# The second normalisation of a two-layer kernel: statistics in halves, turns by tile, rotary products ahead of the last norm, tables loaded earlier

## The chip, the cores and the metric

The kernel runs on 1 core of one Trainium2 chip. The metric is the device time of one execution in microseconds (us), as the median of several runs. Engines: TensorE (PE, with its weight loads PEld), VectorE (DVE), ScalarE (ACT), GpSimd (POOL), and SyncE (SP), which only issues DMAs here. Each engine runs its own instructions in program order; semaphores order them between engines.

## The reference

Input x has 2048 tokens of 128 values. All is fp32.

```
xn = layernorm(x)
x  = x + token_memory(xn) + expert(xn)        # layer 0
xn = layernorm(x)                             # the second norm: this change
x  = x + attention(xn) + ffn(xn)              # layer 1
```

The attention of layer 1 has one head of 128 dimensions. q = xn Wq and k = xn Wk; of each, the first 64 dimensions are turned (rotary embedding) and the last 64 are skipped, that is, taken as they are:

```
even, odd = split(rot)                        # 32 + 32 of the 64 dimensions
rot' = [even*cos - odd*sin, even*sin + odd*cos]
q, k = [rot', skip] / sqrt(128)
p = softmax(q k^T, causal);  out = (p (xn Wv)) Wo
```

The ffn is tanh/silu-gated with two hidden layers of 512 and gelu.

## The kernel before, in words

Tokens stand in 16 tiles of 128, four tiles (512 tokens) make a chunk c = 0..3. Every engine has a hand-written list of steps; the order within an engine is the order in the code, and semaphores (`wait_ge`) are all that holds it against the others. Layer 0 ends at about 77 us with block b of the new x in PSUM bank b. What then happens, with the lines of the profile:

- ScalarE moves block b from PSUM to the tensor `x` (`first_block(b)`, L1247) in the order 1, 0, 2, 3. `x1_ready` counts them.
- VectorE takes the statistics of four tiles (`statistics`, L1905; for chunk 0 straight out of PSUM, L1898), aggregates them (`variances`, L1910); ScalarE takes the root (`deviations`, L1253); VectorE takes the reciprocal (L1916) and the shift -mean/deviation (`shifts`, L1917). Then the chunk is normalised into `xn`: tiles 0 and 1 by ScalarE (`normed`, L1260), tiles 2 and 3 by VectorE (L1922).
- TensorE transposes the four tiles (`normed`, L801), once all four are there, into PSUM; ScalarE copies the result to `xT` (`transposed`, L1264; `xt2_act` counts them).
- TensorE multiplies the chunk (`projected(c)`) with `wturn` (L810), `wswap` (L811: the same dimensions with the halves swapped) and `wskip` (L816). q and k stand side by side in the 128 columns of each.
- VectorE multiplies the first product by the cosine table (L1947) and the second by the sine table (L1949) into the buffer `TURN[c % 2]` (`rope_dve` counts), and adds the halves for q (L1951); GpSimd adds them for k (L1476). ScalarE copies the skipped dimensions (L1292, L1293). Behind it stand the masks in bf16 (L1299, L1300) and the fp16 high half of xT (L1268).
- From then on come the values (L826), and tile by tile the scores (L879), their maximum (L1981, VectorE), the exponential (L1354, ScalarE), the transposes (L892) and the weighted values (L902), with the ffn's gates (TensorE L852 and L853, tanh L1311, VectorE L1966, L1967 and, for most, the cast L1973, GpSimd's residue L1461 and L1462) laid between them by the lists `GATE_EARLY` and `GATE_LATE`. A gate u from 6 on waits for residue u-5 (`gate_low`, L1965). Then come the hidden layers (L929, L930).

Before the norm, SyncE has loaded the weights. It waits for `x1_ready` 2 and loads the tables `cosT` and `sinT`, 1 MB each, into a part of the arena that layer 0 has left by then; at `x1_ready` 4 it loads 1 MB of `h1_T`. GpSimd waits for `x1_ready` 4 too, and then makes fp16 casts of two weights (L1469, L1470) before its first k sum. VectorE computes some small products of scales (L1933 to L1937) between the last norm and the first rotary product.

In `projected(0)` the transposes of chunk 1 stand between the swapped and the skipped product; those of chunks 2 and 3 come after the skipped products of chunks 0 and 1:

```python
            normed(0)
            keep_warm(4, 7)
            for c in range(4):
                ...
                projected(c)
                for n in ((2,), (3,), (), ())[c]:
                    normed(n)
            values(0)
```

Of the kernel before, what the change touches and what calls it, by code (L numbers as in the profile page):

```python
# [6 lines left out]
ALU = mybir.AluOpType  # L7
ACT = mybir.ActivationFunctionType
AX = mybir.AxisListType
# [4 lines left out]
P = 128  # L14
# [72 lines left out]
def program(nc, a, out):  # L87
    with ExitStack() as ctx:
# [42 lines left out]
        s1, s2, sh1, sh2, s1h, s12 = (take(HT4) for _ in range(6))  # L131
        a_tab = at[0]
        HT = take(2 * T).rearrange("p (h t) -> p h t", h=2)
        cosT, sinT = arena[:, a_tab:a_tab + T], arena[:, a_tab + T:a_tab + 2 * T]
        a_blocks = at[0]
# [16 lines left out]
        Gf = take((HALF + 1) * S)  # L152
        G = Gf.rearrange("p (j s) -> p j s", j=HALF + 1)
        CC = take(3 * (L + 1) * L).rearrange("p (q j t) -> p q j t", q=3, j=L + 1)

# [6 lines left out]
        STf = take(SCAN * RW)  # L162
        VC = take(HALF * L).rearrange("p (j t) -> p j t", j=HALF)
        O1, O2, O3, O4, TA, TB, TC = (take(HALF * L).rearrange("p (j t) -> p j t", j=HALF) for _ in range(7))
        Yf = take(L * L)
# [73 lines left out]

        TURN = [hBf[:, T * c:T * c + 2 * BANK].rearrange("p (k t) -> p k t", k=2) for c in range(2)]  # L240
        xd = hBf[:, T + 2 * BANK:T + 3 * BANK]
# [184 lines left out]
        def _(sp):  # L426
# [16 lines left out]

            sp.wait_ge(x1_ready, 2)
            for i, n in enumerate(("cos", "sin")):
                sp.dma_start((cosT, sinT)[i], a[n]).then_inc(tab_in, 16)

# [52 lines left out]
        def _(pe):  # L500
# [293 lines left out]
            def normed(c):  # L794
                b = 4 * ((c + 1) % 2)
                pe.wait_ge(xn2_act, 2 * c + 2)
                pe.wait_ge(xn2_dve, 2 * c + 2)
                if c >= 2:
                    pe.wait_ge(xt2_act, c - 1)
                for n in range(4 * c, 4 * c + 4):  # L800
                    i = tr(PS[:, b, (n % 4) * P:(n % 4 + 1) * P], xn[:, n, :], ident)  # L801
                i.then_inc(xrt_done, 1)

            def projected(c):
                b = 4 * ((c + 1) % 2)
                xc = xT[:, c * BANK:(c + 1) * BANK]
                pe.wait_ge(xt2_act, c + 1)
                if c >= 2:
                    pe.wait_ge(rope_dve, 2 * c - 2)
                mm(bank(b + 2), wturn, xc, start=True, stop=True).then_inc(turn_done, 1)  # L810
                mm(bank(b + 3), wswap, xc, start=True, stop=True).then_inc(turn_done, 1)  # L811
                if c == 0:
                    normed(1)
                if c >= 2:
                    pe.wait_ge(skip_act, 2 * c - 2)
                mm(bank(b + 1), wskip, xc, start=True, stop=True).then_inc(skip_done, 1)  # L816
# [14 lines left out]
            for c in range(4):  # L831
                if c == 1:

                    pe.wait_ge(x1_ready, 4)
                projected(c)
                for n in ((2,), (3,), (), ())[c]:
                    normed(n)
            values(0)
# [174 lines left out]
        def _(act):  # L1013
# [241 lines left out]
            def normed(c):  # L1255

                act.wait_ge(x1_ready, max(c + 1, 2))
                act.wait_ge(shift_ready, c + 1)
                for n in range(4 * c, 4 * c + 2):
                    f(xn[:, n, :], x[:, n, :], ACT.Identity, scale=lnt[:, 1, n:n + 1], bias=lnt[:, 6, n:n + 1]).then_inc(xn2_act, 1)  # L1260
# [8 lines left out]

            first_block(1)  # L1270
            deviations(0)
            first_block(0)
            normed(0)
            first_block(2)
            deviations(1)
            transposed(0)
            first_block(3)
            normed(1)
            deviations(2)
            normed(2)  # L1280
            transposed(1)
            deviations(3)
            normed(3)
            transposed(2)

            f(small[:, 38:39], lnt[:, 0, 12:13], ACT.Tanh)
            for c in range(4):

                b = 4 * ((c + 1) % 2)
                cols = slice(c * BANK, (c + 1) * BANK)  # L1290
                act.wait_ge(skip_done, c + 1)
                f(qT1[0:ROT, cols], PS[0:ROT, b + 1, :], ACT.Copy).then_inc(skip_act, 1)  # L1292
                f(kT1[0:ROT, cols], PS[ROT:P, b + 1, :], ACT.Copy).then_inc(skip_act, 1)  # L1293
                if c == 0:
                    transposed(3)
                if c == 2:
                    act.wait_ge(xt2_act, 1)
                    high(0)
                    f(ident_b, ident, ACT.Copy).then_inc(mask_act, 1)  # L1299
                    f(causal_b, con[:, C_CAUSAL:C_CAUSAL + P], ACT.Copy).then_inc(mask_act, 1)  # L1300
            act.wait_ge(xt2_act, 4)
# [217 lines left out]
        def _(dve):  # L1519
# [380 lines left out]

            def statistics(b):

                dve.wait_ge(x1_ready, b if b == 1 else b + 1)
                for n in range(4 * b, 4 * b + 4):
                    did(v.bn_stats(st[:, n, :], x[:, n, :]))  # L1905
# [13 lines left out]
            def normed(c):  # L1919
                dve.wait_ge(x1_ready, max(c + 1, 2))  # L1920
                for n in range(4 * c + 2, 4 * c + 4):
                    v.tensor_scalar(xn[:, n, :], x[:, n, :], mv[:, n, 0:1], lnt[:, 1, n:n + 1], ALU.subtract, ALU.mult).then_inc(xn2_dve, 1)  # L1922

            first_variances()
            for c in range(4):
                shifts(c)
                normed(c)
                if c < 3:
                    statistics(c + 1)
                    variances(c + 1)  # L1930

            dve.wait_ge(small_in, 16 * 13)
            v.tensor_scalar(s1h, s1, 0.5, None, ALU.mult).then_inc(scales_ready, 1)  # L1933
            v.scalar_tensor_tensor(out=s12, in0=s1, scalar=0.5, in1=s2, op0=ALU.mult, op1=ALU.mult).then_inc(scales_ready, 1)
            need(did(v.tensor_tensor(s12a, s1, s2, ALU.mult)))
            v.tensor_reduce(sums[:, 0:1], s12a, AX.X, ALU.add, apply_absolute_value=True).then_inc(sums_ready, 1)
            v.tensor_reduce(sums[:, 1:2], sh1, AX.X, ALU.add, apply_absolute_value=True).then_inc(sums_ready, 1)  # L1937

            dve.wait_ge(tab_in, 32)
            for c in range(4):  # L1940
                b = 4 * ((c + 1) % 2)
# [6 lines left out]
                dve.wait_ge(turn_done, 2 * c + 2)  # L1948
                v.tensor_tensor(TURN[c % 2][:, 1, :], bank(b + 3), sinT[:, cols], ALU.mult).then_inc(rope_dve, 1)  # L1949
                dve.wait_ge(rope_dve, 2 * c + 2)  # L1950
                v.tensor_tensor(qT1[ROT:P, cols], TURN[c % 2][0:ROT, 0, :], TURN[c % 2][0:ROT, 1, :], ALU.add).then_inc(turned_dve, 1)  # L1951

            def values(c):
# [156 lines left out]
```

## Time and profile before

| what | value |
|---|---|
| runs | 259.75, 259.87, 261.55 us, median 259.87 |
| profiled execution: span from its first to its last instruction | 258.2 us |
| profiled execution: its own time | not listed apart from the span |
| TensorE busy | 245.4 us (95%) |
| VectorE busy | 206.3 us (80%) |
| ScalarE busy | 186.8 us (72%) |
| GpSimd busy | 112.7 us (44%) |
| mean granted TensorE clock | 0.992 of full |
| DMA | 8.50 MB in the whole kernel |

Busy time is the time in which an engine executes; register, semaphore and DMA-issuing instructions don't count. Idle time of an engine costs something only where another one waits for it. Durations overlap where instructions are pipelined: a row with "x2" gives the time from the start of the first to the end of the second. The end of a TensorE instruction is modelled; its starts are recorded.

### The profile page before, as it was taken

How to read it: one execution, taken by the hardware profiler on the slowest of the kernel's cores; microseconds unless marked ns; L12 is line 12 of the kernel's file. 1: busy time of each engine (PE TensorE's matmuls, PEld its weight loads, DVE VectorE, ACT ScalarE, POOL GpSimd, SP SyncE). 2: the span in 40 equal slices, each digit the busy share in tenths (PEclk: the TensorE clock that was granted, in tenths of full speed). 3: DMA queues.
4: the chain of work that ended last, by engine and by line, in shares of the span. 5: the costliest groups of instructions: out<-in, count | busy, mean ns of one | idle time of the engine just before them, and what ended most of it. 6: DMA issues, size and time to landing. Idle time of an engine off the chain costs nothing.

```text
span 258.2 us, 5143 instructions
## 1 busy us (share of the span) xinstructions
PE 245.4 (95%) x1665; PEld 160.8 (62%) x1665; DVE 206.3 (80%) x694; ACT 186.8 (72%) x459; POOL 112.7 (44%) x148
## 2 busy tenths in 40 slices
PE   7798799999999999999999999999999999999993
PEld 2257554567674458688777767976975444444482
DVE  5998789999968898998899896897623897666684
ACT  1588499986637797887757899989923997777730
POOL 9698300000001689988655795987880000000000
PEclk9999799999999999999999999999999999999999
DMA  7720000000004704000000000000000000000004
GB/s 198 198 57 3 0 1 3 1 0 3 1 1 175 316 3 164 3 0 1 4 0 3 0 0 0 5 0 3 0 0 3 0 0 0 3 3 0 0 30 139
DMA packets 8303, 8.50 MB, mean 33 GB/s; under 512 B 1745, under 2 KB 7378, under 8 KB 7762
## 3 DMA queue, kind: packets, MB, share of 16 engines
q1 hardware_dynamic: 7442, 7.65, 9.1%
q10 hardware_dynamic: 832, 0.49, 0.7%
q8 instruction: 15, 0.25, 0.4%
q14 instruction: 14, 0.11, 0.2%
HBM read 7.09 MB, written 1.05 MB: 32 GB/s over the span
## 4 chain that ended last, share of the span: by engine, by line
PE 66%; DVE 16%; POOL 8%; ACT 4%; issue 3%; DMA 2%; DVEq 0%; SPq 0%; POOLq 0%; ACTq 0%
PE PS L930 11%; PE PS L929 11%; PE PS L902 8%; PE PS L879 7%; PE PS L892 4%; POOL arena L1461 4%; POOL arena L1462 3%; PE PS L693 3%; PE PS L646 3%; PE PS L701 2%; DMA x<-L_attn_x 2%; DVE mxb L1981 2%; DVE arena L1967 2%; PE PS L530 2%; PE PS L685 1%
## 5 line engine op out<-in xcount | busy, mean ns | idle before, releaser
L929 PE MATMUL PS<-arena 128*128 128x512 f16 x128 | 48.5, 379 | 0.0
L930 PE MATMUL PS<-arena 128*128 128x512 f16 x128 | 48.5, 379 | 0.0
L2039 DVE TENSOR_TENSOR arena<-arena 128x512 f32<-128x512 f32 x32 | 22.2, 693 | 13.0 <-ACT arena L1385 13.0
L879 PE MATMUL PS<-arena 128*128 128x512 f32 (+3 forms) x80 | 31.9, 530 | 0.3 <-ACT arena L1354 0.3
L1384 ACT ACTIVATE arena<-PS,arena 128x512 f32<-128x512 f32 x32 | 22.9, 716 | 9.1 <-PE PS L930 9.1
L1461 POOL TENSOR_TENSOR arena<-arena 128x256 f32<-128x256 f32 x32 | 21.6, 674 | 15.4 <-DVE arena L1973 12.9
L1354 ACT ACTIVATE arena<-PS,lnt 128x512 f32<-128x512 f32 (+3 forms) x40 | 24.8, 628 | 2.9 <-DVE lnt L1988 2.8
L1462 POOL TENSOR_TENSOR arena<-arena,small 128x256 f16<-128x256 f32 (+1 forms) x36 | 23.8, 662 | 2.8
L1469 POOL CAST arena<-arena 128x512 f16<-128x512 f32 x2 | 1.3, 636 | 54.3 <-ACT x L1247 54.3
L1385 ACT ACTIVATE arena<-PS,arena 128x512 f16<-128x512 f32 x32 | 22.8, 713 | 0.0
L1981 DVE TENSOR_REDUCE mxb<-PS 128x1 f32<-128x512 f32 (+3 forms) x40 | 22.1, 601 | 0.0
L930 PEld LDWEIGHTS PS<-arena 128*128 128x128 f16 x128 | 12.5, 98 | 14.7
L929 PEld LDWEIGHTS PS<-arena 128*128 128x128 f16 x128 | 12.5, 98 | 14.6
L879 PEld LDWEIGHTS PS<-arena 128*128 128x128 f32 x80 | 14.0, 191 | 12.0 <-issue 9.8
L892 PE MATMUL PS<-con,arena 128*128 128x128 f32 x136 | 19.5, 273 | 0.0
L902 PE MATMUL PS<-arena,xn 128*128 128x128 f32 x144 | 19.3, 278 | 0.0
L902 PEld LDWEIGHTS PS<-arena,xn 128*128 128x128 f32 x144 | 17.7, 191 | 1.1 <-ACT xn L1338 0.2
L902 PE MATMUL PS<-arena 128*128 128x128 f32 x128 | 17.3, 278 | 0.6 <-ACT arena L1338 0.6
L2010 DVE SCALAR_TENSOR_TENSOR x<-PS,lnt,x 128x128 f32<-128x128 f32 x16 | 5.6, 351 | 14.2 <-PE PS L902 13.6
L892 PEld LDWEIGHTS PS<-con,arena 128*128 128x128 f32 x136 | 15.1, 141 | 2.7 <-issue 1.9
L902 PEld LDWEIGHTS PS<-arena 128*128 128x128 f32 x128 | 15.6, 191 | 1.3 <-ACT arena L1338 1.0
L1967 DVE SCALAR_TENSOR_TENSOR arena<-PS,arena 128x256 f32<-128x256 f32 x32 | 15.5, 484 | 1.1
(291 smaller groups left out, 615.5 us busy)
## 6 DMA issues: line engine op xcount, KB each, us to landing
arena<-h_T SPq DMA_DIRECT2D x2, 1024.0 KB, 6.3
x<-L_attn_x SPq DMA_DIRECT2D x4, 256.0 KB, 4.7
arena<-cos SPq DMA_DIRECT2D x1, 1024.0 KB, 4.8
arena<-sin SPq DMA_DIRECT2D x1, 1024.0 KB, 7.8
arena<-w_T SPq DMA_DIRECT2D x3, 256.0 KB, 3.3
out<-arena SPq DMA_DIRECT2D x2, 256.0 KB, 2.2
con<-shape_constants ACTq DMA_DIRECT2D x1, 192.5 KB, 3.5
out<-arena SPq DMA_DIRECT2D x1, 192.0 KB, 2.0
```

Of the source, the lines that this page charges most:

```text
L879: i = mm(PS[:, k, 0:cnt * P], qT1[:, t * P:(t + 1) * P], kT1[:, c * P:(c + cnt) * P], start=True, stop=not last)
L892: i = tr(PS[:, 4 + gi % 2, (b - c) * P:(b - c + 1) * P], Pr[t % 2][:, b * P:(b + 1) * P], ident)
L902: i = mm(PS[:, 7, (t % 4) * D:(t % 4 + 1) * D], PT[t % 2][:, b * P:(b + 1) * P], V1[:, b, :], start=(b == 0), stop=(b == t))
L929: mm(bank(b), wH[:, k, m * P:(m + 1) * P], sH[:, k, cols], start=(k == 0), stop=False)
L930: i = mm(bank(b), wL[:, k, m * P:(m + 1) * P], sL[:, k, cols], start=False, stop=(k == HT4 - 1))
L1354: f(Pr[t % 2][:, c * P:(c + cnt) * P], PS[:, SCORE_BANK[gi], 0:cnt * P], ACT.Exp, scale=1.0 / D, bias=nbs[:, t:t + 1], accum_out=rsums[:, ...
L1384: f(FP[u % 4], bank(u % 8), ACT.Gelu, scale=s_[:, u % HT4:u % HT4 + 1])
L1385: f(high, bank(u % 8), ACT.Gelu, scale=s_[:, u % HT4:u % HT4 + 1]).then_inc(read, 1)
L1461: o.need(o.did(tt(rest, value, high, ALU.subtract)))
L1462: return tt(low, rest, low_scale.broadcast_to([P, cols]), ALU.mult)
L1981: i = did(v.tensor_reduce(mxb[:, gi:gi + 1], PS[:, SCORE_BANK[gi], 0:cnt * P], AX.X, ALU.max))
L2039: v.tensor_tensor(RP[m], FP[m], high, ALU.subtract).then_inc(rest_ready, 1)
```

## The change

Seven edits, all around the second norm:

1. `cosT` and `sinT` move to places in the arena that layer 0 leaves earlier; SyncE loads the cosines once `lanes_act` is 8 and the sines once `tables_ready` is 1 and `terms_act` is 2 (in the trace of before, about 34 to 40 us). VectorE waits for both tables before the norm's loop. The buffers `TURN` move to another place.
2. VectorE: two of the next chunk's four statistics stand between the aggregation of a chunk and its reciprocal, where it waits for ScalarE's root; the other two after the chunk's norm. For the last chunk the two rotary products of chunk 0 stand there.
3. VectorE: the rotary sum is a step of its own; the small products of scales come after rotary chunk 1.
4. ScalarE: blocks move in the order 1, 2, 0, 3, and the steps in a new order: each turned block is copied earlier, the skipped copies of chunk 0 come before the last norm.
5. TensorE transposes tile by tile, in the order 2, 0, 3, 1, each with a wait of its own.
6. TensorE: the transposes of chunk c+1 stand between the swapped and the skipped product of chunk c, for c = 0, 1, 2.
7. Waits on `x1_ready` follow the new order of the blocks.

```diff
+        cosT = Gf[:, S:S + T]
...
+        sinT = arena[:, at[0]:at[0] + T]
...
-        TURN = [hBf[:, T * c:T * c + 2 * BANK].rearrange("p (k t) -> p k t", k=2) for c in range(2)]
+        TURN = [hAf[:, 2 * T + 2 * BANK * c:2 * T + 2 * BANK * (c + 1)].rearrange("p (k t) -> p k t", k=2) for c in range(2)]
...
-            sp.wait_ge(x1_ready, 2)
-            for i, n in enumerate(("cos", "sin")):
-                sp.dma_start((cosT, sinT)[i], a[n]).then_inc(tab_in, 16)
+            sp.wait_ge(lanes_act, 8)
+            sp.dma_start(cosT, a["cos"]).then_inc(tab_in, 16)
+            sp.wait_ge(tables_ready, 1)
+            sp.wait_ge(terms_act, 2)
+            sp.dma_start(sinT, a["sin"]).then_inc(tab_in, 16)
...
             def normed(c):
                 b = 4 * ((c + 1) % 2)
-                pe.wait_ge(xn2_act, 2 * c + 2)
-                pe.wait_ge(xn2_dve, 2 * c + 2)
                 if c >= 2:
                     pe.wait_ge(xt2_act, c - 1)
-                for n in range(4 * c, 4 * c + 4):
+                for k in range(4):
+                    n = 4 * c + (2, 0, 3, 1)[k]
+                    pe.wait_ge(xn2_act if k % 2 else xn2_dve, 2 * c + k // 2 + 1)
                     i = tr(PS[:, b, (n % 4) * P:(n % 4 + 1) * P], xn[:, n, :], ident)
...
-                if c == 0:
-                    normed(1)
+                if c < 3:
+                    normed(c + 1)
...
-                for n in ((2,), (3,), (), ())[c]:
-                    normed(n)
```

ScalarE's steps before and after (`skipped(c)` is the pair of copies L1292, L1293; it was a loop over c before):

```
before: block 1, root 0, block 0, norm 0, block 2, root 1, turned 0, block 3,
        norm 1, root 2, norm 2, turned 1, root 3, norm 3, turned 2, tanh (table load),
        skipped 0, turned 3, skipped 1, skipped 2, high 0, masks, skipped 3, high 1
after:  block 1, block 2, root 0, block 0, norm 0, turned 0, root 1, norm 1,
        block 3, root 2, turned 1, norm 2, root 3, skipped 0, turned 2, norm 3,
        tanh (table load), skipped 1, turned 3, skipped 2, high 0, masks, skipped 3, high 1
```

VectorE's after:

```diff
+            first_variances()
+            dve.wait_ge(tab_in, 32)
+            for c in range(4):
+                if c < 3:
+                    statistics(c + 1, 0)
+                else:
+                    rotated(0)
+                shifts(c)
+                normed(c)
+                if c < 3:
+                    statistics(c + 1, 1)
+                    variances(c + 1)
+
+            rotary_sum(0)
+            rotated(1)
+            rotary_sum(1)
+            dve.wait_ge(small_in, 16 * 13)
...
+            for c in range(2, 4):
+                rotated(c)
+                rotary_sum(c)
```

`statistics(b, half)` waits for `x1_ready` 1, 2 or 4 (b = 1, 2, 3) and takes two tiles.

## Rows read from the trace of the kernel before

**Rows 1.** Windows: us, busy by engine (instructions), PEclk, DMA share, GB/s.

```profile
82.30:88.00 5.70, 5.64 (x19) 2.72 (x20) 4.80 (x32) 3.99 (x11) 4.17 (x4) 1.00 1.01 425
96.00:103.00 7.00, 7.00 (x55) 5.83 (x55) 6.03 (x18) 5.23 (x15) 6.41 (x6) 1.00 0.46 151
```

**Rows 2.** The chain that ended last: start, us, engine, tile, line.

```profile
116.66 0.62 POOL arena L1462
...
117.33 0.43 DVE arena L1966
```

**Rows 3.** VectorE (DVE) timeline: start, us, line, operation [idle before <-releaser].

```profile
80.13 0.86 DVE L1905 BATCH_NORM_STATS2 st<-x 128x6 f32<-128x128 f32 x4
81.03 0.38 DVE L1910 BATCH_NORM_AGGREGATE mv<-st 128x2 f32<-128x6 f32 x4
81.78 0.18 DVE L1916 RECIPROCAL lnt<-lnt 128x4 f32<-128x4 f32 x1 [0.36 <-ACT lnt L1253]
...
82.58 0.87 DVE L1905 BATCH_NORM_STATS2 st<-x 128x6 f32<-128x128 f32 x4
...
87.55 0.15 DVE L1934 SCALAR_TENSOR_TENSOR arena<-arena 128x4 f32<-128x4 f32 x1
...
87.94 0.68 DVE L1947 TENSOR_TENSOR arena<-PS,arena 128x512 f32<-128x512 f32 x1
...
89.26 0.68 DVE L1951 TENSOR_TENSOR arena<-arena 64x512 f32<-64x512 f32 x1
...
96.09 0.29 DVE L1981 TENSOR_REDUCE mxb<-PS 128x1 f32<-128x128 f32 x1
...
101.73 0.42 DVE L1966 SCALAR_TENSOR_TENSOR arena<-arena,PS 128x256 f32<-128x256 f32 x1 [0.42 <-ACT arena L1311]
```

**Rows 4.** Timeline of TensorE (PE), the same columns.

```profile
80.55 0.66 PE L801 MATMUL PS<-con,xn 128*128 128x128 f32 x4 [0.42 <-ACT xn L1260]
...
82.28 1.13 PE L810 MATMUL PS<-xT,arena 128*128 128x512 f32 x2 [0.21 <-ACT xT L1264]
...
84.10 0.60 PE L801 MATMUL PS<-con,xn 128*128 128x128 f32 x4
84.54 1.02 PE L816 MATMUL PS<-xT,arena 128*128 128x512 f32 x2
...
92.13 1.02 PE L810 MATMUL PS<-xT,arena 128*128 128x512 f32 x2
...
95.59 0.39 PE L879 MATMUL PS<-arena 128*128 128x128 f32 x2
```

**Rows 5.** Timeline of ScalarE (ACT), the same columns.

```profile
82.13 0.59 ACT L1247 ACTIVATE x<-PS 128x512 f32<-128x512 f32 x1
...
87.14 0.88 ACT L1260 ACTIVATE xn<-x,lnt 128x128 f32<-128x128 f32 x2 [0.50 <-DVE lnt L1917]
...
88.52 1.28 ACT L1286 ACT_TABLE_LOAD   x1
...
89.92 0.58 ACT L1292 ACTIVATE arena<-PS 64x512 f32<-64x512 f32 x1
...
91.14 0.60 ACT L1264 ACTIVATE xT<-PS 128x512 f32<-128x512 f32 x1
```

**Rows 6.** Timeline of GpSimd (POOL), the same columns.

```profile
85.56 1.48 POOL L1470 TENSOR_SCALAR arena<-arena 128x512 f16<-128x512 f32 x1
89.37 1.70 POOL L1476 TENSOR_TENSOR arena<-arena 64x512 f32<-64x512 f32 x1 [2.33 <-DVE arena L1949]
...
97.34 1.17 POOL L1461 TENSOR_TENSOR arena<-xT,arena 128x512 f32<-128x512 f32 x1
```

**Rows 7.** Timeline of VectorE in the attention.

```profile
165.09 1.18 DVE L1973 CAST arena<-arena 128x256 f16<-128x256 f32 x1
```

**Rows 8.** Timeline of GpSimd in the attention.

```profile
164.85 1.28 POOL L1496 TENSOR_TENSOR arena<-arena 128x512 f32<-128x512 f32 x1
```

**Rows 9.** DMA issues: KB each, median us from issue to landing.

```profile
arena<-sin SPq DMA_DIRECT2D x1, 1024.0 KB, 7.8
```

More of the change, by code:

```diff
@@ L131, in program @@
         s1, s2, sh1, sh2, s1h, s12 = (take(HT4) for _ in range(6))
-        a_tab = at[0]
         HT = take(2 * T).rearrange("p (h t) -> p h t", h=2)
-        cosT, sinT = arena[:, a_tab:a_tab + T], arena[:, a_tab + T:a_tab + 2 * T]
         a_blocks = at[0]
@@ L1255, in normed @@
             def normed(c):
-                act.wait_ge(x1_ready, max(c + 1, 2))
+                act.wait_ge(x1_ready, max(c + 1, 3))
                 act.wait_ge(shift_ready, c + 1)
@@ L1268, in high, with skipped @@
                 f(xH[:, c * BANK:(c + 1) * BANK], xT[:, c * BANK:(c + 1) * BANK], ACT.Copy).then_inc(xh_act, 1)
[L1270 to L1287, printed above, removed]
+            def skipped(c):
                 b = 4 * ((c + 1) % 2)
@@ L1293, in _ @@
                 f(kT1[0:ROT, cols], PS[ROT:P, b + 1, :], ACT.Copy).then_inc(skip_act, 1)
[L1294 to L1300, printed above, removed]
+            first_block(1)
+            first_block(2)
+            deviations(0)
+            first_block(0)
+            normed(0)
+            transposed(0)
+            deviations(1)
+            normed(1)
+            first_block(3)
+            deviations(2)
+            transposed(1)
+            normed(2)
+            deviations(3)
+            skipped(0)
+            transposed(2)
+            normed(3)
+            f(small[:, 38:39], lnt[:, 0, 12:13], ACT.Tanh)
+            skipped(1)
+            transposed(3)
+            skipped(2)
+            act.wait_ge(xt2_act, 1)
+            high(0)
+            f(ident_b, ident, ACT.Copy).then_inc(mask_act, 1)
+            f(causal_b, con[:, C_CAUSAL:C_CAUSAL + P], ACT.Copy).then_inc(mask_act, 1)
+            skipped(3)
             act.wait_ge(xt2_act, 4)
@@ L1899, in first_variances, with statistics @@
                 variances(0)
-            def statistics(b):
-                dve.wait_ge(x1_ready, b if b == 1 else b + 1)
-                for n in range(4 * b, 4 * b + 4):
+            def statistics(b, half):
+                dve.wait_ge(x1_ready, (1, 2, 4)[b - 1])
+                for n in range(4 * b + 2 * half, 4 * b + 2 * half + 2):
                     did(v.bn_stats(st[:, n, :], x[:, n, :]))
@@ L1919, in normed, with rotated @@
             def normed(c):
-                dve.wait_ge(x1_ready, max(c + 1, 2))
+                dve.wait_ge(x1_ready, max(c + 1, 3))
                 for n in range(4 * c + 2, 4 * c + 4):
                     v.tensor_scalar(xn[:, n, :], x[:, n, :], mv[:, n, 0:1], lnt[:, 1, n:n + 1], ALU.subtract, ALU.mult).then_inc(xn2_dve, 1)
[L1924 to L1940, printed above, removed]
+            def rotated(c):
                 b = 4 * ((c + 1) % 2)
@@ L1949, in _, with rotary_sum @@
                 v.tensor_tensor(TURN[c % 2][:, 1, :], bank(b + 3), sinT[:, cols], ALU.mult).then_inc(rope_dve, 1)
+            def rotary_sum(c):
+                cols = slice(c * BANK, (c + 1) * BANK)
                 dve.wait_ge(rope_dve, 2 * c + 2)
                 v.tensor_tensor(qT1[ROT:P, cols], TURN[c % 2][0:ROT, 0, :], TURN[c % 2][0:ROT, 1, :], ALU.add).then_inc(turned_dve, 1)
+            first_variances()
[14 more added lines that the diff above has]
+            dve.wait_ge(small_in, 16 * 13)
+            v.tensor_scalar(s1h, s1, 0.5, None, ALU.mult).then_inc(scales_ready, 1)
+            v.scalar_tensor_tensor(out=s12, in0=s1, scalar=0.5, in1=s2, op0=ALU.mult, op1=ALU.mult).then_inc(scales_ready, 1)
+            need(did(v.tensor_tensor(s12a, s1, s2, ALU.mult)))
+            v.tensor_reduce(sums[:, 0:1], s12a, AX.X, ALU.add, apply_absolute_value=True).then_inc(sums_ready, 1)
+            v.tensor_reduce(sums[:, 1:2], sh1, AX.X, ALU.add, apply_absolute_value=True).then_inc(sums_ready, 1)
+            for c in range(2, 4):
+                rotated(c)
+                rotary_sum(c)
             def values(c):
```

## The prediction

> **What bounds the kernel now.** I read the windows of busy time first. From 96 to 103 us TensorE is busy 7.00 of 7.00 us at granted clock 1.00, while VectorE has 6.03 [rows 1]. So what follows the change is TensorE's, with some waits on VectorE, and the changed stretch (77 to 96 us) is worth what it brings forward TensorE's first scores. The chain of waits says otherwise: from 97 to 117 us it runs through GpSimd's residues and then into the gate of line 1966 [rows 2]. I take these links for coincidence. By the code gate u waits for residue u-5. The gate at 117.33 is u = 9 (two gates a tile from tile 2 on), so it wants four residues, and the one that ends at 117.28 is the seventh.
>
> Then the three engines' timelines of the norm. VectorE repeats a pattern every 2.45 us (80.13 to 82.58): four statistics 0.90, four aggregations 0.39, an idle 0.36 while ScalarE takes the root, then reciprocal, shift and two norms 0.80. It goes into the rotary products at 87.94 and takes the first maximum at 96.09 [rows 3]. TensorE's turns and projections start at 82.28 and stand almost back to back until the first scores at 95.59 [rows 4]. Both are thus tight at 96: scores end about 0.45 after their start, just when VectorE has finished.
>
> **VectorE, part by part.** Removed: the idle 0.36 behind each root. Two statistics cost 0.45 and fill it, three times; the first pair of rotary products, 2 x 0.60 by the distance of 87.94 to the next but one at 89.26, fills the fourth. That is 4 x 0.36 = 1.44 at most. Given back: (a) ScalarE now copies chunk 0's turned block before root 1. The turn can end about 80.85 (its last tile is ScalarE's second norm, ready 80.5 [rows 4]), so the 0.60 copy ends 81.45 and the root runs 81.4 to 81.7; VectorE, at 81.4, idles 0.2 to 0.3. (b) Block 3's move out of PSUM now stands behind norm 1 (about 82.9 to 83.5 instead of 82.13 to 82.73 [rows 5]), and VectorE at 83.3 wants it for the first half of chunk 3: 0.15. Together 0.4 to 0.5. So the reciprocal of chunk 3 falls at 86.7 although 1.2 us of rotary work has been done before it (86.67 in the pattern of before), and all VectorE work to the last rotary sum would end at 96.09 - 0.95 = 95.1.
>
> **TensorE.** Before, the four transposes start at 80.55, when ScalarE's last norm is there. Turning by tile leaves one of the four behind it; the four warming matmuls follow at once and chunk 0's projection starts about 81.5 instead of 82.28, with the copy of 80.85 to 81.45 just in time. A chunk then costs 1.82 (82.28 to 84.10, turned and swapped projection) + 0.44 (transposes) + 0.92 (the skipped projection, half of 1.82 and a little) = 3.2 us [rows 4]. Three chunks bring TensorE to 91.1, where it wants the turned block of chunk 3. That block comes from ScalarE.
>
> **ScalarE.** Here I see the end of the gain. Before, the order is norm 3, copy 2, table load at 88.52 (1.28), the two skipped copies of chunk 0 from 89.92, copy 3 at 91.14 [rows 5]. After, it is root 3, skipped copies 0 (85.7 to 87.0), copy 2 (about 87.15), norm 3 (87.65, two of 0.88 together), table load, skipped copies of chunk 1, copy 3. Skipped copies 0 take the place in which ScalarE idled before; norm 3 is 0.5 later than at 87.14, but copy 2 now stands ahead of it and not behind. The table load thus comes at 88.5 as before, and copy 3 at 89.9 + 1.22 = 91.12, as before, ending 91.7. What was late before was TensorE (92.13); now it waits and starts chunk 3 at 91.75. The gain there is 0.38 us of the 0.76 that TensorE had at chunk 0. From there to the scores the work is unchanged (92.13 to 95.59 is 3.46): 95.21. The masks and the high half, behind skipped copies 2, are ready near 94.2, in time.
>
> **GpSimd, and a shared resource.** Line 1476 adds 64 partitions in 1.70 us where line 1461 adds 128 in 1.17; it starts 0.1 after VectorE's own sum of line 1951 (0.68), which has two inputs in SBUF [rows 3, 6]. The difference, 0.53, is about what is left of VectorE's sum. The opposite order shows too: the cast of line 1973 at 165.09 takes 1.18, where line 1966 handles the same 128x256 shape in 0.42 [rows 3], and ends 0.14 after the GpSimd instruction that was running since 164.85 [rows 7, 8]. So whichever comes second waits. Bounds for what the change meets of it: nothing, and one GpSimd addition of 1.17 us for each time that VectorE comes second. It can come second twice. Sum 0 is due at 87.55, while GpSimd's weight casts, 0.7 later than before with block 3, run to 87.75: 0.2. The scale products of lines 1934 and 1935 (two SBUF inputs) stood at 87.5, with GpSimd idle [rows 3]; now they come at 90.5, just when sum 1 lets GpSimd's second addition go: up to 1.15. I take 0.2 and, for the second, most of 1.15; VectorE's 0.95 is then spent, and it reaches the first maximum at about 96.05.
>
> The Trainium skill says this as a rule ("SBUF — State Buffer", Who interferes with whom): a VectorE instruction with two SBUF inputs and a GpSimd instruction that reads SBUF exclude each other, and the first to issue decides. The two rows agree with it; that tiny instructions pay a whole GpSimd instruction is what it adds, and no row of before has it. Without the rule VectorE would be free at 95.1 and wait for the scores.
>
> **The sum.** With no collision all engines pass 96 us 0.38 us earlier, TensorE setting it: VectorE's 0.95 is cut to TensorE's 0.38. With the collisions the first maximum gains only 0.04; but VectorE had a wait of 0.42 at 101.73 on a tanh that itself follows TensorE [rows 3], so it catches up most of TensorE's lead. I take 0.3 us. Behind 102 us everything moves by this, and nothing there changes except the chance phase of VectorE and GpSimd (a cast that waits 0.9 us or not [rows 7]), worth some 0.2 either way by my estimate. The loads are worth nothing: the sine table lands 7.8 us after its issue at 79.6 [rows 9], so at 87.4, covered by the norm (no idle at 87.94), and it is now loaded 40 us earlier. The span was 258.2 us; the runs' median, 259.87, lies 1.67 above it, which I keep (the profiled execution's own time is not listed). 258.2 - 0.3 + 1.67 = 259.57.
>
> **Rivals.**
> 1. ScalarE's order doesn't bind and the stretch gains what VectorE gains: 0.95 to 1.2 us, 258.8. For it: VectorE is the visible chain of this stretch. Against: two engines were tight at 96 us, and copy 3 keeps its place.
> 2. GpSimd takes the port first at sum 0 too. VectorE's sum is ready at 87.55 and GpSimd's next addition may start from 87.85; if VectorE comes more than 0.3 us later than I reckon, sum 0 waits 1.17 more. VectorE then ends at 97.2, 1.1 later than before, of which some 0.4 is caught up at 101.73: 0.5 to 0.9 slower, 260.5. Up to that 0.3 us the change is a gain, from it on a loss. For it: rotary products ahead of norm 3 leave no slack; against: only the phase decides.
> 3. The tables' loads, 2 MB inside the token chain (35 to 45 us), delay its short instructions or their fetching. Two of the three 1 MB loads fill the share of 1.01 that 82.3 to 88 us shows [rows 1], so one takes about 2.8 us, and a fetch behind one could wait as long: 262.6. Against: under that full DMA the copy of line 1247 took 0.59 [rows 5] and VectorE kept its 2.45 us.
> 4. The change doesn't do what it says: the roots are held by ScalarE's copies so that the idle only moves. Then chunk 3 is 0.5 late and copy 3 with it: 260.0.
>
> **How the numbers follow.** Forecast as above 0.55 (its own range 259.2 to 259.8); rival 1 0.17; rival 2 0.13; rival 3 0.05; rival 4 0.10. The 8-in-10 range reaches from near rival 1 to near rival 2: 258.7 to 260.4. One per cent, 2.6 us, is what a measurement of this kernel can tell from no change; only rival 3 reaches it, and no sum of gains does. So faster 0.02, same 0.93, slower 0.05.
>
> **What would show it.** Right: statistics in pairs with no idle of 0.36 behind the aggregations; chunk 0's projection near 81.5; TensorE idle 0.5 to 0.7 before chunk 3's projection, released by ScalarE's line of the turned copy; scores near 95.2; a scale product of over 1 us near 90.5. Wrong: no such idle in TensorE (rival 1), the first rotary sum over 1.5 us long and the first maximum near 97 (rival 2), long instructions or idle at 35 to 45 us (rival 3), recurring idle behind the roots (rival 4).

## The result, and the profile after

| kernel | median of the runs | range | runs |
|---|---|---|---|
| before | 260.06 us | 258.92 to 261.62 | 17 |
| changed | 261.39 us | 261.01 to 262.80 | 17 |

The ratio is 1.0051, with a 95% interval of 1.0031 to 1.0071: the change costs 0.5%, some 1.3 us. The forecast was 259.57 with a range of 258.7 to 260.4: a small gain was expected, and a loss beyond the range came.

The executions of every kernel here fall into groups 1.0 to 1.7 us apart by TensorE's granted clock, which differs ahead of the norm (in the profiles here, 0.91 to 1.00 from 30 to 58 us), so medians are given as well for the "clock group", the runs with a mean clock of 0.9875 to 0.9935. In that group the changed kernel has 261.12 us (9 runs) and the kernel before 259.88 to 260.06 (10 to 22 runs in each set of experiments): 1.1 to 1.2 us. Inside the profiles I count from the norm's first statistics, which leaves out what differs ahead of it.

The tables' loads cost little if anything. They are now issued at 30.77 and 37.82 us and take 4.7 us each, inside the token chain, and the norm starts at 77.43 against 77.46 us before. The granted clock moves that start too, so a fairer pair is the kernel before with late scale products (below), which loads the tables at the old place: its norm starts at 77.25 with a clock of 0.94 from 30 to 58 us, as the changed kernel has it. So up to some 0.2 us can't be ruled out.

The page of the changed kernel, its head and its busy times:

```profile
span 259.3 us, 5142 instructions
...
PE 245.9 (95%) x1665; PEld 160.0 (62%) x1665; DVE 208.5 (80%) x694; ACT 186.8 (72%) x459; POOL 112.0 (43%) x148
```

VectorE is busy 2.2 us longer than before with the same 694 instructions. So some instructions took longer, and the timeline of VectorE shows where (start, us, line, operation, shapes; the lines to compare are [rows 3]):

```profile
78.65 0.45 DVE L1909 BATCH_NORM_STATS2 st<-x 128x6 f32<-128x128 f32 x2
...
84.24 0.98 DVE L1926 TENSOR_SCALAR xn<-x,mv,lnt 128x128 f32<-128x128 f32 x2
...
85.94 0.66 DVE L1936 TENSOR_TENSOR arena<-PS,arena 128x512 f32<-128x512 f32 x1
86.52 0.68 DVE L1938 TENSOR_TENSOR arena<-PS,arena 128x512 f32<-128x512 f32 x1
87.11 0.17 DVE L1920 RECIPROCAL lnt<-lnt 128x4 f32<-128x4 f32 x1
...
88.02 1.66 DVE L1944 TENSOR_TENSOR arena<-arena 64x512 f32<-64x512 f32 x1
89.72 0.69 DVE L1936 TENSOR_TENSOR arena<-PS,arena 128x512 f32<-128x512 f32 x1
...
91.04 0.68 DVE L1944 TENSOR_TENSOR arena<-arena 64x512 f32<-64x512 f32 x1
91.76 1.12 DVE L1963 TENSOR_SCALAR arena<-arena 128x4 f32<-128x4 f32 x1
...
97.25 0.29 DVE L2001 TENSOR_REDUCE mxb<-PS 128x1 f32<-128x128 f32 x1
...
102.76 0.42 DVE L1986 SCALAR_TENSOR_TENSOR arena<-arena,PS 128x256 f32<-128x256 f32 x1 [0.42 <-ACT arena L1315]
```

The idle of 0.36 us behind the aggregations is filled, as it was meant to be (78.65 stands in it; only ahead of chunk 1's reciprocal 0.33 is left), and the reciprocal of chunk 3 comes at 87.11. But three rows are too long. The first rotary sum takes 1.66 us; the same instruction at 91.04 takes 0.68. The first scale product, 128x4 elements, takes 1.12 where it took 0.16 before. The pair of norms at 84.24 takes 0.98 where it takes 0.60 elsewhere, and the next instruction starts 0.90 behind it instead of 0.51. These are 0.98, 0.96 and 0.38 us more, together 2.3 for the 2.2 of the page. Beside them stands the timeline of GpSimd of the same kernel:

```profile
84.27 1.50 POOL L1474 TENSOR_SCALAR arena<-arena 128x512 f16<-128x512 f32 x1
...
86.31 1.48 POOL L1474 TENSOR_SCALAR arena<-arena 128x512 f16<-128x512 f32 x1
87.88 1.26 POOL L1480 TENSOR_TENSOR arena<-arena 64x512 f32<-64x512 f32 x1
91.08 1.76 POOL L1480 TENSOR_TENSOR arena<-arena 64x512 f32<-64x512 f32 x1 [1.95 <-DVE arena L1938]
```

The k sum of 87.88 started 0.14 us before VectorE's q sum of 88.02 and ran to 89.14; that of 91.08 started just behind VectorE's sum of 91.04, took half a microsecond longer than the first and ran to 92.84, and the scale product issued at 91.76 ended at 92.88. VectorE ends its rotary work at 97.22 instead of 96.07 and takes the first maximum at 97.25 instead of 96.09.

The timelines of TensorE and ScalarE in the changed kernel:

```profile
81.54 1.11 PE L813 MATMUL PS<-xT,arena 128*128 128x512 f32 x2
...
92.13 1.13 PE L813 MATMUL PS<-xT,arena 128*128 128x512 f32 x2 [0.72 <-ACT xT L1265]
...
95.70 0.39 PE L880 MATMUL PS<-arena 128*128 128x128 f32 x2
...
98.48 0.30 PE L893 MATMUL PS<-con,arena 128*128 128x128 f32 x1 [0.67 <-DVE arena L1975]
```

```profile
86.06 0.30 ACT L1254 ACTIVATE lnt<-mv,small 128x4 f32<-128x4 f32 x1 [0.71 <-DVE mv L1914]
...
88.86 1.28 ACT L1296 ACT_TABLE_LOAD   x1
...
91.48 0.60 ACT L1265 ACTIVATE xT<-PS 128x512 f32<-128x512 f32 x1
```

TensorE starts chunk 0's projection 0.74 earlier than before [rows 4] and has lost all of it at chunk 3, for whose turned block from ScalarE it waits 0.72. The scores come at 95.70, 0.1 later than before. Then it waits 0.67 more at 98.48, for VectorE's copy of the values. The gate at 102.76 is 1.03 later than in [rows 3], counted from the norm 1.06, and it stays so: the last of this line's 32 instructions starts at 187.43, 1.08 after the 186.35 of the kernel before.

### The profile page after: what moved, and what is told of

It is laid out like the page before. It is cut to its first block, busy times and chain, and to the rows that moved or that the text cites. A ratio compares the mean times of both kernels' runs of the same rounds, so it can differ in the third digit from the quotient of the medians.

```text
span 259.3 us, 5142 instructions
## 1 busy us (share of the span) xinstructions
PE 245.9 (95%) x1665; PEld 160.0 (62%) x1665; DVE 208.5 (80%) x694; ACT 186.8 (72%) x459; POOL 112.0 (43%) x148
## 4 chain that ended last, share of the span: by engine, by line
PE 71%; DVE 17%; ACT 6%; issue 2%; DMA 2%; SPq 0%; DVEq 0%; ACTq 0%
PE PS L930 11%; PE PS L931 11%; PE PS L903 9%; PE PS L880 9%; PE PS L893 5%; PE PS L695 3%; PE PS L648 3%; DVE arena L1987 2%; PE PS L703 2%; DVE arena L1986 2%; DMA x<-L_attn_x 2%; DVE mxb L2001 2%; PE PS L854 2%; PE PS L853 2%; PE PS L532 2%
```

## The experiments

Two theories stood against each other. PORT: VectorE and GpSimd hold each other up for whole instructions, and the new order has put three of VectorE's instructions second. (The name is a label: the traces show the waits, not a port.) ORDER: the new order on ScalarE and TensorE makes the last turned block late, and VectorE's delay only follows. In the tables "max" is the first maximum of the scores, "gate" the first gate product, both in us from the norm's first statistics in the one profiled execution, "end" the end of the span counted so; "median" is that of the runs in the clock group named above. Every ratio is against the kernel before, run in the same set.

| kernel | scores | max | gate | end | median (runs) |
|---|---|---|---|---|---|
| before | 18.13 | 18.63 | 24.27 | 180.74 | 259.9 to 260.06 |
| changed | 18.27 | 19.82 | 25.33 | 181.87 | 261.12 (9) |
| changed, scale products early | 18.26 | 18.75 | 24.40 | 181.31 | 260.74 (6) |
| changed, k sum second | 18.26 | 18.98 | 24.56 | 181.21 | 260.53 (6) |
| changed, products behind the norm | 18.27 | 19.51 | 25.02 | 181.63 | 260.87 (9) |
| before, scale products late | 18.13 | 19.71 | 25.22 | 181.85 | 261.09 (6) |
| both repairs | 18.26 | 18.74 | 24.40 | 181.28 | 260.48 (7) |
| both, new ScalarE order | 17.37 | 17.85 | 23.54 | 179.84 | 259.00 (7) |
| ... and early weight casts | 17.07 | 17.55 | 23.23 | 180.04 | 259.31 (6) |
| ... and GpSimd 0.3 us later | 17.07 | 17.55 | 23.23 | 179.66 | 258.93 (7) |
| both, new order, products behind | 18.00 | 18.48 | 24.17 | 180.54 | 259.75 (6) |

The experiments are of three sets on three chips, and in each the kernel before has a median of its own: 260.06 for the four kernels under "changed", 259.90 for the next three, 259.88 for the last two. Distances between sets are best read from these.

**The kernel before, with one edit.** The five scale products move from ahead of rotary chunk 0 to behind rotary chunk 1. Nothing else of the change is in it.

```diff
-            dve.wait_ge(small_in, 16 * 13)
-            v.tensor_scalar(s1h, s1, 0.5, None, ALU.mult).then_inc(scales_ready, 1)
...
                 v.tensor_tensor(qT1[ROT:P, cols], TURN[c % 2][0:ROT, 0, :], TURN[c % 2][0:ROT, 1, :], ALU.add).then_inc(turned_dve, 1)
+                if c == 1:
+                    dve.wait_ge(small_in, 16 * 13)
+                    v.tensor_scalar(s1h, s1, 0.5, None, ALU.mult).then_inc(scales_ready, 1)
...
```

> The kernel before with one edit: the scale products stand behind the sum of rotary chunk 1 instead of ahead of chunk 0. The work is the same. PORT: the first of them waits for GpSimd's second k sum, 1.0 to 1.1 us, first maximum at 97.1, total 0.8 to 1.1 over the kernel before. ORDER: within 0.2 of the kernel before.

Measured: 261.12 us, ratio 1.0036 (1.0009 to 1.0063); in the clock group 1.03 over the kernel before. First the row of the kernel before, then VectorE and GpSimd of this one:

```profile
87.48 0.16 DVE L1933 TENSOR_SCALAR arena<-arena 128x4 f32<-128x4 f32 x1
```

```profile
90.74 0.69 DVE L1944 TENSOR_TENSOR arena<-arena 64x512 f32<-64x512 f32 x1
91.46 1.12 DVE L1947 TENSOR_SCALAR arena<-arena 128x4 f32<-128x4 f32 x1
92.50 0.15 DVE L1948 SCALAR_TENSOR_TENSOR arena<-arena 128x4 f32<-128x4 f32 x1
...
96.96 0.29 DVE L1981 TENSOR_REDUCE mxb<-PS 128x1 f32<-128x128 f32 x1
```

```profile
90.79 1.77 POOL L1476 TENSOR_TENSOR arena<-arena 64x512 f32<-64x512 f32 x1 [0.27 <-DVE arena L1942]
```

The same scale product of 0.16 us takes 1.12 as soon as it stands behind a q sum, with nothing else changed. Its end and GpSimd's (90.79 + 1.77 = 92.56) tell the mechanism: it ends 0.02 after GpSimd. This single move costs the kernel before nearly as much as the whole change does. The wait on GpSimd is thus shown, and shown to be enough for such a loss; ORDER had expected at most 0.2.

**The changed kernel, scale products early.** They move into VectorE's wait for `count_done`, ahead of the norm, where GpSimd is idle.

```diff
+            dve.wait_ge(small_in, 16 * 13)
+            v.tensor_scalar(s1h, s1, 0.5, None, ALU.mult).then_inc(scales_ready, 1)
...
             dve.wait_ge(count_done, 1)
```

> The changed kernel, its five small scale products moved ahead of the norm, into VectorE's wait for the last count of layer 0. Theory PORT (whichever of VectorE and GpSimd comes second waits for the other's whole instruction): the scale product of 1.12 us and the 0.4 us behind it leave the stretch, VectorE is free 1.5 us earlier, so at 95.7, and the first maximum falls to the scores' end, about 96.2 instead of 97.25; total 0.9 to 1.1 us under the changed kernel, so 0.2 to 0.4 over the kernel before. Theory ORDER (the new order on ScalarE and TensorE makes the last turned block late, and VectorE's delay is only a follower): scores stay at 95.7, and the gain is at most the 0.46 us of moved work.

Measured: 260.77 us, ratio 1.0027 (1.0001 to 1.0053). VectorE in this kernel, whose norm starts at 76.39:

```profile
86.97 1.67 DVE L1951 TENSOR_TENSOR arena<-arena 64x512 f32<-64x512 f32 x1
...
95.14 0.29 DVE L2001 TENSOR_REDUCE mxb<-PS 128x1 f32<-128x128 f32 x1 [0.37 <-PE PS L882]
...
100.79 0.42 DVE L1986 SCALAR_TENSOR_TENSOR arena<-arena,PS 128x256 f32<-128x256 f32 x1 [0.42 <-ACT arena L1315]
```

The maximum is at the scores' end, 18.75 from the norm, and the gate is 0.93 earlier than in the changed kernel, as PORT had it, although the q sum still takes 1.67. But the total is only 0.4 to 0.6 better, not the 0.9 to 1.1 expected: against the kernel before, the maximum of tile 6 is 0.13 late and that of tile 7 is 0.57. The cause is taken up below.

**The changed kernel, k sum second.**

```diff
                 pool.wait_ge(rope_dve, 2 * c + 2)
+                pool.wait_ge(turned_dve, c + 1)
                 tt(kT1[ROT:P, cols], TURN[c % 2][ROT:P, 0, :], TURN[c % 2][ROT:P, 1, :], ALU.add).then_inc(turned_pool, 1)
```

> The changed kernel, GpSimd's k sum of a chunk held until VectorE's q sum of that chunk is done. PORT: the first q sum takes 0.68 instead of 1.66 us; GpSimd's sums take about 1.2 instead of 1.8 us, so GpSimd loses nothing. The scale products then stand at 90.7, with GpSimd's second sum just let go: still one wait of about 1 us there. First maximum about 96.3, total 0.7 to 1.0 under the changed kernel. ORDER: no gain, as GpSimd only starts later.

Measured: 260.66 us, ratio 1.0024 (0.9993 to 1.0055), 0.59 under the changed kernel in the clock group, where 0.7 to 1.0 was expected. VectorE and GpSimd:

```profile
87.98 0.69 DVE L1945 TENSOR_TENSOR arena<-arena 64x512 f32<-64x512 f32 x1
...
90.74 0.17 DVE L1964 TENSOR_SCALAR arena<-arena 128x4 f32<-128x4 f32 x1
90.82 0.15 DVE L1965 SCALAR_TENSOR_TENSOR arena<-arena 128x4 f32<-128x4 f32 x1
90.89 1.24 DVE L1966 TENSOR_TENSOR small<-arena 128x4 f32<-128x4 f32 x1
...
96.37 0.29 DVE L2002 TENSOR_REDUCE mxb<-PS 128x1 f32<-128x128 f32 x1
```

```profile
88.84 1.27 POOL L1481 TENSOR_TENSOR arena<-arena 64x512 f32<-64x512 f32 x1 [1.10 <-DVE arena L1945]
90.85 1.26 POOL L1481 TENSOR_TENSOR arena<-arena 64x512 f32<-64x512 f32 x1 [0.74 <-DVE arena L1945]
```

GpSimd's sum takes 1.27 instead of 1.77 us when it doesn't overlap VectorE's. The explicit wait isn't free for GpSimd, though: its sum ends 1.41 to 1.44 us behind VectorE's, against 1.13 in the kernel before. The q sum is back at 0.69. Of the scale products the first two slip through before GpSimd starts at 90.85; the third (`s1 * s2`, two inputs in SBUF), issued 0.04 after it, takes 1.24. That the same scale product right behind a q sum takes 0.17 here also rules out that it waits for the q sum itself. The wait was expected; that it falls on whichever instruction comes after GpSimd's start, on one with two SBUF inputs here and on one with a single input in the other runs, is what these two runs show together.

**The changed kernel, rotary products of chunk 0 behind the last norm.**

```diff
-                else:
-                    rotated(0)
...
+            rotated(0)
             rotary_sum(0)
```

> The changed kernel, the rotary products of chunk 0 back behind the last norm. PORT: the q sum comes right behind its products, before GpSimd, and takes 0.68 us; VectorE loses the filled root wait of 0.4 but gains 1.0: first maximum 96.6 or better, total 0.4 to 0.8 under the changed kernel. ORDER: total unchanged or 0.4 over the changed kernel.

Measured: 260.87 us, ratio 1.0011 (0.9987 to 1.0036); in the clock group 0.25 under the changed kernel, less than the 0.4 to 0.8 expected. VectorE:

```profile
86.44 0.33 DVE L1921 SCALAR_TENSOR_TENSOR lnt<-mv,lnt 128x4 f32<-128x4 f32 x1
86.70 1.02 DVE L1926 TENSOR_SCALAR xn<-x,mv,lnt 128x128 f32<-128x128 f32 x2
...
88.52 0.68 DVE L1944 TENSOR_TENSOR arena<-arena 64x512 f32<-64x512 f32 x1
...
91.28 1.13 DVE L1962 TENSOR_SCALAR arena<-arena 128x4 f32<-128x4 f32 x1
```

The q sum is at 0.68 and the scale product still waits (1.13), both as expected. The last norm's pair now takes 1.02 beside GpSimd's weight work of 86.15. That row looks worse than it is, for the next instruction starts 0.51 behind it, as behind any pair. Most of what eats the gain of 0.98 is that VectorE sits idle 0.37 for the last root again, and that the shift ahead of the norm takes 0.33 instead of 0.16 beside GpSimd, which delays the norm by 0.18.

**Both repairs.** Scale products early and k sum second together.

> The changed kernel with both repairs: scale products ahead of the norm and GpSimd's k sum behind VectorE's q sum. PORT: VectorE is free near 94.7 instead of 97.22 and waits for the scores, which stay at 95.7 because TensorE waits for the last turned block; first maximum about 96.2, at most 0.1 from the run with the scale products moved alone. So the 1.0 us of the q sum is worth nothing once TensorE is the last. Behind it a difference of up to 0.5 from the phase of GpSimd. ORDER: the same. This run tells what bounds the stretch once the collisions are gone.

Measured: 260.56 us, ratio 1.0028 (1.0000 to 1.0056); one of its twelve executions took 362.86 us at a mean granted clock of 0.654, why is not known, and of the numbers here it is only in the 260.56. Maximum and gate are those of the run with the scale products alone, to 0.01. VectorE is free at 95.55 (its last rotary sum starts at 94.86 and takes 0.69; 94.7 was expected) and the scores are what it waits for. So the second microsecond was hidden behind TensorE: the two waits of 1.0 us on VectorE did not add, and each repair alone recovers 0.77 and 0.93 of the 1.06 at the gate. What is left is 0.13 at the gate, which is TensorE's late scores (0.13, too), and 0.4 more at tile 6. So even without these two waits the changed kernel is no faster than the kernel before: the 0.38 us that TensorE was to gain isn't there either.

**Both repairs and a new order on ScalarE.**

```diff
-            skipped(1)
             transposed(3)
+            skipped(1)
```

> Both repairs, and on ScalarE the copy of the last turned block ahead of the skipped copies of chunk 1. If TensorE's wait of 0.72 before chunk 3 is the bound that is left, the scores come 0.6 to 0.8 earlier than in the run with both repairs, at about 95.0, the maximum at about 95.5, and the total falls 0.4 to 0.8 under the kernel before, less what the phase of GpSimd takes. If something else bounds (the skipped copies, the masks), nothing moves.

Measured: 259.25 us, ratio 0.9985 (0.9955 to 1.0015). This interval shows no difference; in the clock group it is 259.00 us (7 runs, 258.87 to 259.28) against 259.90 (13 runs, 259.70 to 260.07), without overlap. TensorE and ScalarE (this profile's norm starts at 78.86):

```profile
92.67 1.11 PE L813 MATMUL PS<-xT,arena 128*128 128x512 f32 x2
...
96.23 0.39 PE L880 MATMUL PS<-arena 128*128 128x128 f32 x2
```

```profile
90.28 1.28 ACT L1296 ACT_TABLE_LOAD   x1
...
92.01 0.60 ACT L1265 ACTIVATE xT<-PS 128x512 f32<-128x512 f32 x1 [0.23 <-PE PS L804]
```

TensorE's wait before chunk 3 is gone, and scores come 0.89 earlier than with both repairs, somewhat more than the 0.6 to 0.8 expected; the cast at tile 6, taken up below, gives back another 0.44. ORDER, dead as a cause of the loss, is thus the cause of the missing gain: two copies of 0.6 us stood between the table load and the block for which TensorE waited.

**Early weight casts.** On top of that:

```diff
-            pool.wait_ge(x1_ready, 4)
+            pool.wait_ge(x1_ready, 1)
             for wH, wL, w in ((w1H, w1L, w1T), (w2H, w2L, w2T)):
```

> As the run before it, and GpSimd's weight casts released by the first moved block instead of the fourth, so at 77.9 instead of 83.7. PORT: VectorE's first norm of chunk 2 loses its wait (0.98 for the pair instead of 0.60), root 3 and all behind it come 0.4 earlier, unless the casts now hit the norm of chunk 0 or 1 instead. Expect 0.1 to 0.4 us under the run before it; if the casts only move the collision, no difference.

Measured: 259.93 us, ratio 0.9987 (0.9957 to 1.0017). The gate is 0.31 earlier and the pair of norms is back at 0.60, as expected; yet the total is 0.2 (by the end in the profile) to 0.3 us (by the clock group) worse than in the run before. Outside the clock group the medians of the two kernels are equal (260.65 and 260.64), so the traces carry the argument here and not the medians. The norms of chunks 0 and 1, which now stand beside the casts, take 0.63 and 0.60, so the collision was not moved to them. The loss is again at tile 6, where VectorE casts for the first time. VectorE, and GpSimd at that moment:

```profile
85.47 0.60 DVE L1934 TENSOR_SCALAR xn<-x,mv,lnt 128x128 f32<-128x128 f32 x2
...
120.31 0.80 DVE L1994 CAST arena<-arena 128x256 f16<-128x256 f32 x1
```

```profile
120.28 0.67 POOL L1465 TENSOR_TENSOR arena<-arena 128x256 f32<-128x256 f32 x1
```

The cast, issued 0.03 us after GpSimd had started, takes 0.80. In the kernel before, the same cast took its least:

```profile
120.16 0.29 DVE L1973 CAST arena<-arena 128x256 f16<-128x256 f32 x1
```

```profile
119.67 0.61 POOL L1462 TENSOR_TENSOR arena<-arena,small 128x256 f16<-128x256 f32 x1
120.43 0.67 POOL L1461 TENSOR_TENSOR arena<-arena 128x256 f32<-128x256 f32 x1
```

It was issued when GpSimd's instruction had 0.12 us left. Over the nine kernels seen so far, the first cast takes 0.29 (before), 0.38 (changed), 0.73 (scale products early), 0.58 (k sum second), 0.40 (products behind), 0.40 (before, scales late), 0.73 (both), 0.29 (new order) and 0.80 us (early casts). In the seven that take more than 0.29 it ends 0.15 to 0.16 us after the GpSimd instruction that was running when it was issued, and the maxima from tile 7 on move by what the cast takes over 0.29, to 0.02 us.

**GpSimd 0.3 us later.** A tiny memset ahead of GpSimd's first gate residue of 256 columns, which then starts 0.29 us later from the norm.

```diff
+            pool.wait_ge(xl_ready, 4)
+            o.need(o.did(nc.gpsimd.memset(zd[:, 0:16], 0.0)))
             for t in range(NT):
                 for u in (*GATE_EARLY[t], *GATE_LATE[t]):
                     gate_parts(u)
```

> The run with the early casts, and one tiny memset on GpSimd ahead of its first gate residue, which only makes GpSimd later, by 0.1 to 0.3 us. PORT, applied to the attention: VectorE's first cast (tile 6) came 0.03 us after a GpSimd instruction had started and took 0.80 instead of 0.29; now it comes first, takes 0.29 to 0.4, and the 0.47 us lost there are kept: total 0.3 to 0.5 under the run with the early casts, 0.9 to 1.1 under the kernel before. Rival: the loss at tile 6 has to do with the position of the whole stretch (instruction fetch, scores); then a later GpSimd changes nothing, or costs its 0.1 to 0.3.

Measured: 258.98 us, ratio 0.9972 (0.9940 to 1.0004); in the clock group 258.93 us (7 runs, 258.90 to 259.15) against 259.88 (10 runs, 259.76 to 260.14). VectorE's cast and GpSimd:

```profile
119.09 0.29 DVE L1996 CAST arena<-arena 128x256 f16<-128x256 f32 x1
```

```profile
118.59 0.61 POOL L1466 TENSOR_TENSOR arena<-arena,small 128x256 f16<-128x256 f32 x1
119.35 0.67 POOL L1465 TENSOR_TENSOR arena<-arena 128x256 f32<-128x256 f32 x1
```

An added instruction on GpSimd made the kernel 0.38 us faster, in the profile and in the medians alike, as was expected; the cast is back at 0.29 and nothing ahead of it moved (the gate is at 23.23 in both). It is the fastest kernel of this study, 0.95 us under the kernel before and 2.2 under the changed one. The delay is a demonstration, not a repair: another change ahead of it would move the phase again.

**Are the early products worth anything?** Both repairs and the new order, with chunk 0's products behind the last norm.

> The run with both repairs and ScalarE's new order, with the rotary products of chunk 0 back behind the last norm. VectorE loses the filled root wait, 0.4 us; TensorE's third chunk waits for those products' bank: in the run with the products behind it started 0.5 later for it. Expect scores 0.4 to 0.6 later than in the run with both repairs and the new order, total 0.3 to 0.6 over it, still at or under the kernel before. If the early products are worth nothing, no difference.

Measured: 259.77 us, ratio 1.0003 (0.9975 to 1.0032), in the clock group 0.75 over the same kernel with early products (expected 0.3 to 0.6), and the scores come 0.63 later. TensorE, and VectorE ahead of it:

```profile
87.51 1.10 PE L813 MATMUL PS<-xT,arena 128*128 128x512 f32 x2 [0.80 <-DVE arena L1946]
```

```profile
85.32 0.33 DVE L1929 SCALAR_TENSOR_TENSOR lnt<-mv,lnt 128x4 f32<-128x4 f32 x1
```

TensorE waits 0.80 before chunk 2 until VectorE has read the products of chunk 0 out of PSUM. Not all of this is the place of the products: VectorE idles 0.36 for the root, and the shift again takes 0.33 beside GpSimd and delays the norm by 0.18. That leaves the early products worth most of the difference, since they fill the root's wait and set TensorE's buffers free, and in the changed kernel they cost by what they moved behind them.

## Why the prediction was wrong

- **VectorE, removed idle.** Right in kind: statistics fill the root waits, the idle of 0.3 before the reciprocal of chunk 1 and that of 0.16 on block 3 are there. The step "the reciprocal of chunk 3 falls at 86.7" came out at 87.11. Missing was the pair of norms at 84.24, 0.38 longer beside GpSimd's weight work; I had looked for such waits only at the two later instructions. The run with early casts brings it back to 0.60.
- **"Sum 0 is due at 87.55 ... 0.2".** This step failed. The sum was issued at 88.02, and GpSimd's sum had started at 87.88. Rival 2 had named this point: VectorE more than 0.3 us late. It was 0.47 late, of which 0.38 is the held norm, and the wait was 0.98. I gave 13% to a case that hung on 0.3 us at the end of a sum of a dozen terms, which in hindsight was too little. But this step alone doesn't make the sign: in the run with the k sum second the sum takes 0.69, and the kernel is still 0.47 us slower than the kernel before.
- **"For the second, most of 1.15".** Right in size: 0.96 over the normal length. The waiter was the first scale product, with one input in SBUF, not one of the two I had named for their two inputs. The Trainium skill ("SBUF — State Buffer", Who interferes with whom) has the exclusion both for two SBUF inputs and for `copy`, `cast` and `tensor_scalar` in two-port modes. The runs agree with the first (1.24 us for the product of two SBUF inputs) and with the second for the single-input product (1.12) and the cast (0.80), while the norms' `tensor_scalar` was held in some places and not in others; I had weighed only the first for the scale products.
- **"It catches up most".** Failed. The 0.42 before the first gate is still there in the changed kernel, at 102.76: it follows a tanh, which follows TensorE's gate, and TensorE stands in line behind the values, for which it now waits 0.67 on VectorE. That idle was no slack. Of the 1.19 us by which VectorE came late to the first maximum, counted from the norm, 1.06 are left at the gate and 1.13 at the end.
- **ScalarE and TensorE, "0.38 us earlier".** This step failed in size, and it took the gain away even where nothing collides. The mechanism was right: copy 3 stands behind the table load and the skipped copies, TensorE waits (0.72, forecast 0.5 to 0.7), and the run with the new order removes the wait and gains 0.89. The size was off: copy 3 came at 91.48, not 91.12, since root 3 came 0.4 us late behind the held norm (without the hold, in the run with early casts, the gate is 0.31 earlier), and TensorE's first projection behind its wait was 0.1 us slower to follow than before (0.96 against 0.86 to the next). So TensorE's forecast gain of 0.38 was a loss of 0.1, and the run with both repairs, where the q sum and the scale products wait for nothing, ends 0.54 behind the kernel before and not 0.38 ahead: 0.13 from the scores and some 0.4 from the cast at tile 6.
- **GpSimd's links in the chain.** That the chain of the kernel before ran through GpSimd by coincidence fits the runs: with GpSimd later by 0.3 us a kernel of the same structure got faster. What I called "chance phase, worth some 0.2 either way" is worth up to 0.5 (the cast at tile 6 takes 0.29 to 0.80).
- **The tables.** The sine table was issued at 79.98, not at 79.6, so it landed at 87.8 and not 87.4; its product starts at 88.54 and didn't wait for it. Nothing hangs on it.
- **Rivals.** Rival 1 was out while ScalarE's order stood. Rival 2 is what happened at VectorE, priced at 0.5 to 0.9 for a measured 1.1 to 1.3. Rival 3: at most 0.2 us, by the start of the norm. Rival 4: the roots' idle did go, but its second half, a late copy 3, came true by another cause (the held norm).

In short: four terms of the sum were wrong together. The collision at sum 0 was 0.98 and not 0.2, the one at the norm was not in the sum, TensorE's 0.38 did not come, and the wait at the first gate gave nothing back. The collisions overlap each other and TensorE's delay, so the shares don't add up to the 1.1 us.

## What to carry to other kernels

Where VectorE and GpSimd both work out of SBUF, plan for them to hold each other up: before VectorE's instructions are reordered, look what GpSimd starts at that moment, let the shorter or the critical instruction go first by an explicit wait, and keep tiny instructions out of the stretch altogether, since they can wait as long as large ones. Busy time that grows with the same count of instructions is a sign of it in the profile's page. And an idle that follows a chain back to the engine one has just delayed is not slack.

## What the runs showed of the hardware

- A VectorE instruction issued during a GpSimd instruction that reads SBUF may end only with it: a 128x4 `tensor_scalar` took 1.12 us instead of 0.16, a 128x4 `tensor_tensor` of two SBUF inputs 1.24 instead of 0.15, a 128x256 cast 0.29 to 0.80 by its distance to GpSimd's end (where it was held, it ended 0.15 to 0.16 us behind that). The profile books the wait as busy time of the waiter, not as idle.
- Not every instruction waits: the rotary product at 86.52 of the changed kernel (one input in PSUM, one in SBUF) took its 0.68 and the statistics at 85.14 their 0.47 while GpSimd ran. The norms (`tensor_scalar`, 128x128) are in between: beside the same GpSimd work a pair took 0.60, 0.98 or 1.02, only the 0.98 held up the instruction behind it, and why one waits and the next doesn't stays open.
- It works in both directions: GpSimd's k sum takes 1.77 us behind VectorE's q sum and 1.27 without it. Holding it back by a semaphore until the q sum is done lets it end 0.3 us later than the overlap does.
